# Moving the next chunk's layer norm inside the gated feed-forward loop of a local transformer, on one core

## What is computed

```python
h = shift_token(x)                      # the upper 128 features come from the token before
mu = h.mean(-1, keepdims=True); var = h.var(-1, keepdims=True)
h = (h - mu) / jnp.sqrt(var + 1e-05) * lg + lb
h = h @ w1 + b1                         # 256 -> 2 x 682
a, g = jnp.split(h, 2, axis=-1)
h = a * jax.nn.gelu(g, approximate=False)
x = x + h @ w2 + b2                     # 682 -> 256
```

## Time and profile before

| what | value |
|---|---|
| time, median of 3 runs | 3649.62 us (3648.28 to 3649.73) |
| the profiled execution's own time | 3648.28 us |
| its span, first to last instruction | 3646.5 us |
| PE busy | 3335.7 us (91%) |
| DVE busy | 2204.5 us (60%) |
| ACT busy | 1904.8 us (52%) |
| POOL busy | 150.7 us (4%) |
| granted TensorE clock, mean | 0.957 of full speed |
| feed-forward stage, layer 0 | about 3039.5 to 3179.3 us of the span |
| feed-forward stage, layer 1 | about 3497.1 to 3636.9 us of the span |

### The profile page before, as it was taken

The page is one execution under the profiler, slowest core; times in us unless marked ns, Lnnn a source line. Parts: engine busy times, 40 slices in busy tenths (PEclk is TensorE's granted clock), DMA queues, the critical chain, the costliest instruction groups (busy, mean ns, idle before and its releaser), DMA issues. The chain is left out here.

```text
span 3646.5 us, 51449 instructions
## 1 busy us (share of the span) xinstructions
PE 3335.7 (91%) x19248; PEld 1572.6 (43%) x19248; DVE 2204.5 (60%) x2594; ACT 1904.8 (52%) x2377; POOL 150.7 (4%) x183
## 2 busy tenths in 40 slices
PE   3999999999999999999999687999968997879968
PEld 2333333343333333433333573222235775757757
DVE  5677777776777777777778643000026665556655
ACT  3454554544545545455455115999944762246632
POOL 0000000000000000000000101000002111011110
PEclk8999999999999999999999798999988997989989
DMA  1000000000000000000000001000010000100000
GB/s 47 7 1 6 2 1 7 1 5 4 1 6 2 1 6 3 5 3 1 1 2 1 27 33 54 22 15 21 15 51 1 1 1 29 38 14 1 1 30 24
DMA packets 21497, 44.57 MB, mean 12 GB/s; under 512 B 4655, under 2 KB 15490, under 8 KB 20098
## 3 DMA queue, kind: packets, MB, share of 16 engines
q1 hardware_dynamic: 21250, 41.23, 3.4%
HBM read 35.36 MB, written 5.83 MB: 11 GB/s over the span
## 5 line engine op out<-in xcount | busy, mean ns | idle before, releaser
L627 ACT ACTIVATE a_probs<-PS 128x1024 f32<-128x1024 f32 x928 | 901.8, 1023 | 712.4 <-PE PS L471 710.6
L482 PE MATMUL PS<-a_probs,a_V 128*64 128x512 f32 x3712 | 897.0, 605 | 0.0
L703 DVE TENSOR_TENSOR a_prob_sums<-a_prob_sums,a_probs 128x1024 f32<-128x1024 f32 x512 | 627.5, 1226 | 223.5 <-ACT a_probs L627 196.2
L700 DVE SCALAR_TENSOR_TENSOR a_prob_sums<-a_probs,a_valid,a_prob_sums 128x1024 f32<-128x1024 f32 x384 | 492.7, 1283 | 89.6 <-ACT a_probs L627 65.3
L482 PEld LDWEIGHTS PS<-a_probs,a_V 128*64 128x64 f32 x3712 | 225.7, 136 | 463.1 <-issue 339.1
L1240 ACT ACTIVATE c_probs<-PS 128x1024 f32<-128x1024 f32 (+1 forms) x416 | 402.1, 1022 | 36.4 <-PE PS L1182 27.0
L471 PE MATMUL PS<-a_Q_hi,a_K_hi 64*128 64x512 f16 x1856 | 359.3, 384 | 0.2 <-ACT a_probs L627 0.2
L471 PE MATMUL PS<-a_Q_hi,a_K_lo 64*128 64x512 f16 x1856 | 354.1, 378 | 0.0
L471 PE MATMUL PS<-a_Q_lo,a_K_hi 64*128 64x512 f16 x1856 | 354.1, 378 | 0.0
L471 PEld LDWEIGHTS PS<-a_Q_hi,a_K_hi 64*128 64x128 f16 x1856 | 89.9, 94 | 342.6 <-ACT a_probs L627 183.1
L1182 PE MATMUL PS<-c_Qop,c_Kop 128*128 128x512 f16 (+1 forms) x832 | 219.0, 385 | 18.1 <-DMA c_Qop<-q_part 15.9
(11 more groups left out here) (300 smaller groups left out, 4034.7 us busy)
## 6 DMA issues: line engine op xcount, KB each, us to landing
c_Qop<-q_part SPq DMA_DIRECT2D x64, 64.0 KB, 2.2
d_tables<-in_rotary_dram SPq DMA_DIRECT2D x2, 1792.0 KB, 11.4
c_Kop<-k_part SPq DMA_DIRECT2D x64, 50.0 KB, 2.0
d_wqkv<-in_l1f_wqkv_dram SPq DMA_DIRECT2D x2, 1536.0 KB, 7.8
f_w<-in_l1f_w_dram SPq DMA_DIRECT2D x2, 1536.0 KB, 5.9
X<-in_x_dram SPq DMA_DIRECT2D x1, 2048.0 KB, 8.1
out_dram<-X SPq DMA_DIRECT2D x4, 512.0 KB, 3.6
c_cT<-in_ctxT_dram SPq DMA_DIRECT2D x1, 1601.0 KB, 6.6
```

The lines of the kernel that those rows point to most:

```text
L482: last = nc.tensor.matmul(m.PS[64 * h:64 * h + 64, PVB + c % 2, :], V[e][:, s, 64 * h:64 * h + 64], probs[n % 4][:, h * BANK:(h + 1) * BAN ...
L627: nc.scalar.activation(probs[n % 4][:], m.PS[:, b0:b0 + 2, :].rearrange("p b c -> p (b c)"), ACT.Exp).then_inc(exped, 1)
L700: nc.vector.scalar_tensor_tensor(out=sums, in0=new, scalar=valid[:, s:s + 1], in1=sums, op0=ALU.mult, op1=ALU.add).then_inc(summed, 1)
L703: nc.vector.tensor_tensor(sums, sums, new, ALU.add).then_inc(summed, 1)
```

## The change

Three things change, for both layers.

- At the start of a layer only chunk 0 is normalized. `shift_half(1)`, `move_shifted(1)`, `root(1)`, `statistics(1)` and `stage(1)` leave the start, and `copy_first_half(1)` on POOL goes behind the six splits of w1.
- The layer norm of chunk c + 1 is made inside the loop turn of chunk c, for c = 0, 1 and 2: the shift product at the head of the turn, the transposes between tiles 3 and 4. On ACT the copy and the root go between the gelus of tiles 1 and 2. On DVE the statistics go ahead of the gate of tile 2, and the normalizing behind it.
- Nothing of the layer norm stands around `lower(c)` any more, and the shift product always uses bank 6.

The diff, cut to its core:

```diff
-SHIFT_BANKS, H_BANK, DOWN_BANK = (6, 5, 6, 6), 6, 4
+SHIFT_BANK, H_BANK, DOWN_BANK = 6, 6, 4
...
 # GpSimd
                 copy_first_half(0)
-                copy_first_half(1)
                 pool.wait_ge(s["w1_hi"], l + 1)
                 for t in range(GT):
                     take_lo(nc.gpsimd, w1_lo[:, :, :, t, :], w1[:, :, :, t, :], w1_hi[:, :, :, t, :]).then_inc(s["w1_split"], 1)
+                copy_first_half(1)
...
 # TensorE
                 shift_half(0)
-                shift_half(1)
                 turn_h(0)
                 raise_tiles(0, range(LEAD))
                 for c in range(CH):
+                    if c + 1 < CH:
+                        shift_half(c + 1)
                     raise_tiles(c, range(LEAD, GT - 2))
-                    if c == 0:
-                        turn_h(1)
+                    if c + 1 < CH:
+                        turn_h(c + 1)
                     raise_tiles(c, range(GT - 2, GT))
                     if c + 1 < CH:
                         raise_tiles(c + 1, range(LEAD))
-                    if c + 2 < CH:
-                        shift_half(c + 2)
                     lower(c)
-                    if c + 2 < CH:
-                        turn_h(c + 2)
...
 # ScalarE
                 move_shifted(0)
-                move_shifted(1)
                 root(0)
                 act.wait_ge(s["w1_in"], 48 * (l + 1))
                 move_h(0)
-                root(1)
                 for t in range(LEAD):
                     gelu(0, t)
                 for c in range(CH):
+                    if c + 1 < CH:
+                        move_shifted(c + 1)
+                        root(c + 1)
                     for t in range(LEAD, GT - 2):
                         gelu(c, t)
-                    if c == 0:
-                        move_h(1)
+                    if c + 1 < CH:
+                        move_h(c + 1)
...
-                    if c + 2 < CH:
-                        move_shifted(c + 2)
-                        root(c + 2)
-                        move_h(c + 2)
...
 # VectorE
                 split_h(0)
-                statistics(1)
-                stage(1)
                 for t in range(LEAD):
                     gate(0, t)
                 for c in range(CH):
-                    for t in range(LEAD, GT - 2):
+                    if c + 1 < CH:
+                        statistics(c + 1)
+                    for t in range(LEAD, GT - 3):
                         gate(c, t)
+                    if c + 1 < CH:
+                        stage(c + 1)
+                    gate(c, GT - 3)
                     if c + 1 < CH:
                         split_h(c + 1)
...
-                    if c + 2 < CH:
-                        statistics(c + 2)
-                        stage(c + 2)
                     output(c)
```

More of the change, by code:

```diff
@@ L1755, in shift_half @@
                 def shift_half(c):
-                    if c > 1:
-                        after(pe, "h_moved", base + c)
-                    nc.tensor.matmul(m.PS[:, SHIFT_BANKS[c], :], shift[:, 0, :], Z[:, 4 * c:4 * c + 4, P:D],
+                    after(pe, "h_moved", base + c)
+                    nc.tensor.matmul(m.PS[:, SHIFT_BANK, :], shift[:, 0, :], Z[:, 4 * c:4 * c + 4, P:D],
                                      start=True, stop=False)
                     first = 1 if c == 0 else 0
-                    nc.tensor.matmul(m.PS[:, SHIFT_BANKS[c], first * P:BANK], shift[:, 1, :],
+                    nc.tensor.matmul(m.PS[:, SHIFT_BANK, first * P:BANK], shift[:, 1, :],
                                      Z[:, 4 * c + first - 1:4 * c + 3, P:D], start=False, stop=True).then_inc(s["shifted"], 1)
@@ L1823, in move_shifted @@
                     act.wait_ge(s["shifted"], base + c + 1)
-                    nc.scalar.activation(shifted[c % 2][:, :, P:D], m.PS[:, SHIFT_BANKS[c], :].rearrange("p (j n) -> p j n", n=P),
+                    nc.scalar.activation(shifted[c % 2][:, :, P:D], m.PS[:, SHIFT_BANK, :].rearrange("p (j n) -> p j n", n=P),
                                          ACT.Copy).then_inc(s["shift_moved"], 1)
```

## The result

The changed kernel takes 3681.41 us in the median of four runs (3677.41 to 3683.49), the kernel before 3648.95 (3644.87 to 3649.73). The ratio is 1.009, with an interval of 1.0073 to 1.0107: slower by 0.9%, some 32.5 us. The forecast was 3684, slower. The profiled execution of the changed kernel took 3678.82 us with a span of 3677.0; its mean granted clock was 0.955, that of before 0.957.

What follows compares the result with a forecast made beforehand. PE's work was taken to bound the feed-forward stages from the first tile on, without waits. Start 0.2, shift products 3.4, stalls 22.1 and clock 9.0 sum to 34.7 us over the median 3649.62: 3684 us, range 3671 to 3696.

Steps and rivals of the forecast that it cites:

- The start: Stage start before the first tile: removing chunk 1's work gains nothing; POOL's later copy costs 0.1 us a layer, 0.2 in all.
- One more shift product: In PE's busy part: chunk 1's shift product moves in from the idle start, 1.71 us once per layer, 3.4 us.
- The chain: Shift product to transposes in turns 0, 1, 2: DVE's gate holds the normalizing, PE stands 3.68 us, six times, 22.1 us.
- s: Start of the shift product in a loop turn; the forecast put PE's arrival at s + 7.31, the transposes at s + 10.99.
- No second stall, nothing given back: In the loop: split and gate of tile 4 ready about 1 us before PE wants them; no later PE wait absorbs the stall.
- The clock: Behind each of the six stalls: one slow stretch of PE's granted clock, 1.5 us each, 9.0 us; bounds 0 and 18.
- The sum: Whole kernel: start, shift products, chain and clock together add 34.7 us, giving 3684 us, slower by 0.95%.
- the sum that kept the row: Root to gelu on ACT: trace's 1.31 us per table change, no drain; the page's drain would add 8.1 us (rival, 0.06).
- the one with no stall: Rival, 0.05: normalizing ahead of tile 2's gate ends at s + 6.85; transposes don't wait, only 3.6 us remain.
- The one in which the clock stays up: Rival, 0.20: behind the stalls the clock stays up or falls briefly; sum 25.7 us, time about 3675.
- The rival with two slow stretches: Rival, 0.12: two slow stretches follow each stall if PE is sparse again; sum 43.7 us, time about 3693.

Runs made afterwards that it cites:

- the first experiment: Changed kernel with DVE's normalizing of chunk c + 1 ahead of the gate of tile 2 instead of behind it: 3654.17 us against 3648.60, ratio 1.0011.
- the fourth experiment: Kernel before with only chunk 1's layer-norm step moved into turn 0, chunks 2 and 3 left in place: 3659.76 us against 3648.60, measured once.
- The experiment with the filled stall: Changed kernel with 14 unread matmuls into a free bank, ahead of the transposes of each turn: 3667.37 us against 3648.60, ratio 1.0051.
- without the second table: Changed kernel with the gelu replaced by the identity, so one table does: 3666.83 us, measured once.
- two edits of one engine's order: Kernel before with DVE normalizing chunk 0 ahead of w1's cast, and w2 cast behind the first two gates: 3631.17 us against 3648.86, ratio 0.9946.
- the last experiment: Kernel of the first experiment with chunk 0 normalized ahead of w1's cast and w2 cast behind the first two gates: 3638.99 us against 3648.86, ratio 0.9974.

## Why the prediction was right

The direction, the place and the size of each large term held; that the sum came out so near is in part luck, as the last two steps show. By its own steps:

- **The start**, 0.2 forecast. The first tile comes 24.35 and 25.02 us into the stage, before 24.57 and 24.76. GpSimd's second copy ran at 3529.62 for 0.60 us, and DVE's normalizing of chunk 0, from 3530.18, lasted 1.38 as before. The term is nothing, and so was the gain, as said.
- **One more shift product**, 1.71 each. In the rows of the changed kernel it is 3546.43 to the second matmul of the tile behind at 3548.38, less one matmul of 0.23: 1.72.
- **The chain**, s + 10.99. Copy, root and gelu came where the forecast put them, to 0.01. The gate and its split held the reciprocal for 1.85, not 2.04 (3553.69 to 3555.54), a scrap shorter than in the row where another gate came next, and the hand-over from DVE to PE took 0.05, not 0.10. That makes s + 10.75. Against PE's s + 7.31 the missing work is 3.44 a turn and 20.6 in all, where 22.1 was forecast: the one term that was sized a little too large. The first experiment shows the cause by taking it away, the fourth shows it in one chunk alone.
- **No second stall, nothing given back.** In the faster turn, 31.40 = 27.91 + 3.44 and 0.05 over. Chunk 1's turn in the fourth experiment is followed by turns of 27.9.
- **The clock**, 9.0. The six waits had six slow stretches, but as one, one, two, one, none, one. The experiment with the filled stall gives 1.53 for each, so 9.2, less 1.5 because the last wait in layer 1 no longer had one. The mean of one was right, but nothing in the working gave it: that each stall has exactly one, as the forecast put it, was not so.
- **The sum.** 3.4 + 20.6 + 9.2 − 1.5 = 31.7 us, and the two stages are longer by 17.73 + 14.54 = 32.3. The span grew by only 30.5, because the attention between the two stages took 315.36 instead of 317.46. There too it is the clock: by the granted clock in the traces, 44.4 us of it ran at the lower level before and 41.0 after. The stretch that is gone is the one right ahead of layer 1's stage, before:

```profile
3493.00:3494.00 1.00, 1.00 (x3) 0.82 (x4) 0.00 (x0) 0.00 (x0) 0.00 (x0) 0.50 0.00 0
```

The other profiles agree: with 41.0 us at the lower level the same attention took 315.4 to 315.6 us, with 44.4 it took 317.5 to 318.2, with 54.6 321.3 and with 58.0 323.2 to 323.7. So the two stages are not the only place where these kernels differ, as the text ahead of the prediction had it and the forecast took over. That the change itself took this stretch away is not shown, with one profile of the kernel before. Set against the 31.7, the forecast of 34.7 lay 1.5 too high in the chain, 1.5 too high in the last wait's clock and 0.2 in the start, and was 0.2 too low for the stretches in the turns.

The rule of the Trainium skill on table changes ("ScalarE: Activation LUTs", section "What ACT_TABLE_LOAD costs") names a drain of about 1.38 us beside the load. No run shows it at this place: the root ends at 3551.59 and the gelu starts at 3552.90, 1.31 us later, of which 1.28 are the load, and without the second table the wait shrank by 1.42. Its load agrees, its drain doesn't, and the sum that kept the row was the better one.

Of the rivals, the one with no stall came true in the first experiment, under the condition that it named. The one in which the clock stays up came true in the filled stall, at 3667 against its 3675. Some 6 of these 8 us have a cause: the chain was 1.5 shorter than forecast, the clock stayed up behind both last waits, which before were slow, some 3.0, the start cost nothing instead of 0.2, and the kernel before took 1.0 less beside this run. The rival with two slow stretches came true at one of the six stalls, though PE was at work in them; the condition that it named, PE sparse again after the stall as in the attention, wasn't needed, and in the attention's stretch too PE was busy in the whole of the microsecond 3454.

## What to carry to other kernels

A step that is moved between two tiles of a pipeline has to be followed down each engine's queue, with all that stands ahead of it there; the sum of that chain, against the work that the bounding engine still has, gives the stall to a quarter of a microsecond. Before giving up on such a position, look whether a short link can go ahead of a long one in time in which its engine waits anyway: here that one line of order was worth 27 us. And where the busy part has no wait, look at the start: two edits of one engine's order there gave 17.7 us.

## What the runs showed of the hardware

- The clock doesn't follow from the length of the wait alone. The same 2.08 us wait ahead of the last lowering product was followed by the slow clock in both layers before, in layer 0 only after the change, and in neither layer of the kernel with the normalizing first, of the filled one and of the one without a second table. Waits of 3.2 to 3.3 were followed by it in five of six places, at the same five in two runs, and in both places of the kernel with only chunk 1 moved. Waits of 1.8 to 1.9 never were, in six places, while the two of 2.20 in the last experiment were. So something beside the wait decides; what it is was not tried.
- A slow stretch cost 1.53 us of the 1.7 that 3.4 us at half speed would be, and in one place two followed each other directly (3148.0 to 3154.8). The first of them began 0.9 us before the wait ended; from 3148.90 on PE was at work:

```profile
3148.00:3149.00 1.00, 0.10 (x1) 0.10 (x2) 1.00 (x4) 0.00 (x0) 0.00 (x0) 0.50 0.00 0
3149.00:3150.00 1.00, 1.00 (x5) 1.00 (x6) 0.93 (x3) 0.00 (x0) 0.00 (x0) 0.50 0.00 0
3151.00:3152.00 1.00, 1.00 (x4) 0.71 (x3) 0.00 (x0) 1.00 (x2) 0.00 (x0) 0.50 0.00 0
```

- A DVE operation of 128x4 elements, 0.16 us by itself, lasted 1.04 to 1.25 us beside GpSimd's 128x512 splits and up to 3.47 beside the one of 128x1536. A long operation of GpSimd can so make a stall of PE, by way of DVE. The Trainium skill, "SBUF — State Buffer", section "SBUF: two separate sides", has DVE and GpSimd lock a shared port pair against each other for a whole instruction, where the DVE operation has two inputs in SBUF, as this one has, and GpSimd's reads SBUF. The rows agree, with durations that go up with the size of the split.
